# Last feed-forward of a graph network as one stage: scores as a row on TensorE, ranks between the chunks, weights last, stores by chunk

## The reference

```python
xn = _layernorm(x)                      # no gain, no bias
weights = (xn @ wr + br)[..., 0]        # one score per node
k = max(1, int(0.5 * s)); kk = k - 1    # 1561 nodes chosen
_, idx = jax.lax.top_k(weights, k)
sel_idx = idx[:, :kk]
h = jax.nn.gelu(sel @ w1 + b1)          # sel: the chosen rows of xn
y = (h @ w2 + b2) * weights[sel_idx]
x = x + (zeros.at[sel_idx].set(y) + xn)
```

## Time and profile before

| what | value |
|---|---|
| time, median of 3 executions | 7272.29 us (7267.86 to 7276.22) |
| the profiled execution: its own time, and its span | 7262.79 us, 7261.1 us |
| first instruction of the last feed-forward | 6856.65 us |
| part of the span from there | 404.5 us |
| TensorE busy over the span, mean granted clock | 4243.7 us, 0.806 |
| VectorE busy over the span | 3507.8 us |

### The profile page before, as it was taken

One profiled execution on the slowest core, in us unless ns is written; L12 is line 12 of the kernel. 1 busy time (PEld: TensorE's weight loads), 2 busy tenths in 40 slices (PEclk: granted clock), 3 DMA queues, 4 the chain that ended last, 5 costly groups with the idle time before them and its releaser, 6 DMA issues. The chain is left out here.

```text
span 7261.1 us, 68529 instructions
## 1 busy us (share of the span) xinstructions
PE 4243.7 (58%) x17811; PEld 2977.3 (41%) x17811; DVE 3507.8 (48%) x8561; ACT 1885.5 (26%) x4934; POOL 2998.9 (41%) x3029
## 2 busy tenths in 40 slices
PE   0022567777775693766664843554439964676428
PEld 0000334444443572334443642343228852454315
DVE  6800578888887313436453034632361115554461
ACT  0000056666664120023342110000012211443201
POOL 0677033333331364046662734666104433665200
PEclk9985678888887796878876976776759986988759
DMA  1001033333332373233334322334315642332200
GB/s 38 3 17 27 9 90 100 96 100 97 98 99 55 118 212 103 102 122 89 91 91 61 100 58 89 92 92 92 39 38 174 189 134 75 90 88 79 33 21 18
DMA packets 361250, 602.13 MB, mean 83 GB/s; under 512 B 119031, under 2 KB 245096, under 8 KB 357376
## 3 DMA queue, kind: packets, MB, share of 16 engines
q0 software_dynamic: 162496, 359.47, 20.5%
q1 hardware_dynamic: 198386, 238.43, 10.1%
HBM read 518.82 MB, written 78.64 MB: 82 GB/s over the span
## 5 line engine op out<-in xcount | busy, mean ns | idle before, releaser
L1665 POOL DMA_INDIRECT g0e_got<-g_table,g0e_rc x496 | 474.2, 956 | 1071.0 <-DVEq L1825 730.2
L1418 POOL DMA_INDIRECT g1e_got<-g_table,g1e_rc x496 | 491.0, 990 | 525.0 <-DMA g1e_rc<-rec_dst 294.1
L1418 POOL DMA_INDIRECT g2e_got<-g_table,g2e_rc x496 | 478.5, 965 | 338.8 <-issue 140.7
L1418 POOL DMA_INDIRECT g3e_got<-g_table,g3e_rc x440 | 430.9, 979 | 357.7 <-issue 117.4
L1474 PE MATMUL g2e_pa<-g2e_got,g2e_placew 128*125 128x256 f32 x992 | 341.8, 507 | 376.1 <-DVEq L1576 186.5
L250 POOL DMA_INDIRECT rec_dst<-bydst_rc,bydst_sloti x391 | 402.8, 1030 | 296.0 <-DVEq L442 175.4
L2628 PE MATMUL f_p<-f_w2s,f_hid 128*128 128x256 f32 (+1 forms) x2176 | 498.8, 386 | 43.4 <-ACT f_hid L2648 35.0
L1753 PE MATMUL g0e_spread<-g0e_expanded,g0e_by_tile 128*125 128x512 bf16 x992 | 417.1, 510 | 177.3 <-ACT g0e_spaced L1702 141.6
L2617 PE MATMUL f_p<-f_xt,f_w1s 128*128 128x256 f32 (+1 forms) x2176 | 493.7, 384 | 20.0 <-DMA f_b2s<-in_L_ffn_b 8.0
L1702 ACT ACTIVATE g0e_spaced<-g0e_spread 125x512 bf16<-125x512 f32 x992 | 499.4, 627 | 20.6 <-remote 7.4
L2648 ACT ACTIVATE f_hid<-f_p,f_b1s 128x256 f32<-128x256 f32 (+1 forms) x544 | 251.7, 471 | 861.0 <-PE f_p L2617 493.6
(11 more groups left out here) (656 smaller groups left out, 8265.3 us busy)
## 6 DMA issues: line engine op xcount, KB each, us to landing
f_w1s<-in_L_ffn_W SPq DMA_DIRECT2D x32, 1024.0 KB
f_w2s<-in_L_ffn_W SPq DMA_DIRECT2D x32, 1024.0 KB
g_table<-g1t_out SPq DMA_DIRECT2D x25, 1000.0 KB
f_w1s<-in_L_ffn_w SPq DMA_DIRECT2D x40, 512.0 KB
f_w2s<-in_L_ffn_w SPq DMA_DIRECT2D x40, 512.0 KB
f_results<-f_y SPq DMA_DIRECT2D x72, 256.0 KB
f_b2s<-in_L_ffn_b SPq DMA_DIRECT2D x80, 128.0 KB
f_rows<-XN SPq DMA_DIRECT2D x3, 3125.0 KB
```

Of the source, the lines that this page charges most:

```text
L1418: pool.indirect_dma_start(got[:, g % GOTS, j, :], None, table, bass.IndirectOffsetOnAxis(rc[:, g * GT + j, idx:idx + 1], 0))\
L1665: pool.indirect_dma_start(got[:, s, j, :], None, table, bass.IndirectOffsetOnAxis(rc[:, sl, j, R_IDX:R_IDX + 1], 0)).then_inc(got_in[s], 16)
```

## The change

The stages after the normalization become one block, `scored_experts_stage`, which also stores the result.

- All six loads are issued by SyncE in a small block ahead of `normalize_stage`.
- `wr` is spread over 125 identical columns (`wide`), so that a matmul with `wide` stationary and 500 columns of `XNT` moving leaves the row of 500 scores in each of 125 partitions: 14 matmuls in 7 chunks. VectorE adds the bias and writes `row`. The transpose and the way over DRAM are gone.
- `G` is taken out of `row` by a product with the identity, repeated 25 times, and a sum over each tile.
- TensorE starts the expert once all of `row` is out of PSUM. Between its chunks 0 to 4 VectorE places five tiles each (`place`: the rank instructions of before, and the `X += XN` of that tile), and then takes the chunk's four results with b2 into `XN` (`take`).
- After chunk 4 is taken the ranks are closed and `G` is masked; `settle` does `X += G * XN` for each tile. Chunks 5 and 6 are taken and settled tile by tile.
- SyncE stores each chunk of X when it is settled: six DMAs of 500 KB and one of 125 KB.
- The chunks are written out; there is no loop.

The removed lines of the rank computation, which stand in the function printed above, are cut here.

```diff
--- before.py
+++ after.py
@@ -3270,88 +3270,187 @@
                 pairs(dve, NT, add)
 
 
-def fourth_feed_forward(nc, R, a):
-    CAP = max(1, int(0.5 * N))
-    CHOSEN = CAP - 1 if CAP > 1 else 1
+def scored_experts_stage(nc, R, a, out, CHOSEN):
     F3 = a["L3_ffn_w1"].shape[1]
+    NF = F3 // 128
+    NQ = NCH + 1
+    RANKS = -(-NT // (NQ - 2))
     with ExitStack() as ctx:
         def sb(n, shape, dt=F32):
             return ctx.enter_context(nc.sbuf_tensor(f"f3_{n}", shape, dt))
 
...
+        w1s = sb("w1s", [128, KC, F3])
+        w2s = sb("w2s", [128, NF, D])
+        b1s = sb("b1s", [128, NF])
+        b2s = sb("b2s", [P, D])
+        wide = sb("wide", [128, KC, P])
+        G = sb("G", [P, NT])
+        row = sb("row", [P, N])
...
+        hid = sb("hid", [128, NF, CHUNK])
+        router_in, experts_in = sem("router_in"), sem("experts_in")
+        with nc.Block() as block:
+            @block.sync
+            def _(sp):
+                sp.dma_start(wr[:, :], a["L3_ffn_wr"]).then_inc(router_in, 16)
+                sp.dma_start(br[:, :], row_of(a["L3_ffn_br"], P)).then_inc(router_in, 16)
+                sp.dma_start(w1s[:, :, :], a["L3_ffn_w1"].rearrange("(c k) f -> k c f", k=128)).then_inc(experts_in, 16)
+                sp.dma_start(w2s[:, :, :], a["L3_ffn_w2"].rearrange("(c k) d -> k c d", k=128)).then_inc(experts_in, 16)
+                sp.dma_start(b1s[:, :], a["L3_ffn_b1"].rearrange("a k c -> (a k) c")).then_inc(experts_in, 16)
+                sp.dma_start(b2s[:, :], row_of(a["L3_ffn_b2"], P)).then_inc(experts_in, 16)
         normalize_stage(nc, R, "f3ln", R.X, R.XN)
-        add_stage(nc, [(R.X, R.XN)])
...
+        p1 = [ctx.enter_context(nc.psum_tensor(f"f3_p1{k}", [128, 512], F32)) for k in range(4)]
+        p2 = [ctx.enter_context(nc.psum_tensor(f"f3_p2{k}", [P, 512], F32)) for k in range(4)]
+        widened, scored, rowed, first, acted, second, taken, summed, stored = (sem(n) for n in (
+            "widened", "scored", "rowed", "first", "acted", "second", "taken", "summed", "stored"))
+        chunk = [(q * CHUNK, min(4, NT - 4 * q)) for q in range(NQ)]
+        with nc.Block() as block:
+            @block.tensor
+            def _(pe):
+                pe.wait_ge(widened, 1)
+                for q, (at, tiles) in enumerate(chunk):
+                    n = tiles * P
+                    if q >= 4:
+                        pe.wait_ge(rowed, q - 3)
+                    for c in range(KC):
+                        last = pe.matmul(p1[q % 4][0:P, 0:n], wide[:, c, :], R.XNT[:, c, at:at + n], start=(c == 0),
+                                         stop=(c == KC - 1))
+                    last.then_inc(scored, 1)
+                pe.wait_ge(experts_in, 64)
+                pe.wait_ge(rowed, NQ)
+                for q, (at, tiles) in enumerate(chunk):
+                    n = tiles * P
+                    for f in range(NF):
+                        m = q * NF + f
+                        if m >= 4:
+                            pe.wait_ge(acted, m - 3)
+                        for c in range(KC):
+                            last = pe.matmul(p1[f % 4][:, 0:n], w1s[:, c, f * 128:(f + 1) * 128], R.XNT[:, c, at:at + n],
+                                             start=(c == 0), stop=(c == KC - 1))
+                        last.then_inc(first, 1)
+                    pe.wait_ge(acted, (q + 1) * NF)
+                    for j in range(tiles):
+                        t = 4 * q + j
+                        if t >= 4:
+                            pe.wait_ge(taken, t - 3)
+                        for f in range(NF):
+                            last = pe.matmul(p2[j][:, 0:D], hid[:, f, j * P:(j + 1) * P], w2s[:, f, :], start=(f == 0),
+                                             stop=(f == NF - 1))
+                        last.then_inc(second, 1)
+            @block.scalar
+            def _(act):
+                act.wait_ge(experts_in, 64)
+                for q, (at, tiles) in enumerate(chunk):
+                    n = tiles * P
+                    if q > 0:
+                        act.wait_ge(second, 4 * q)
+                    for f in range(NF):
+                        act.wait_ge(first, q * NF + f + 1)
+                        act.activation(hid[:, f, 0:n], p1[f % 4][:, 0:n], ACT.Gelu_apprx_tanh, bias=b1s[:, f:f + 1])\
+                            .then_inc(acted, 1)
+            @block.vector
+            def _(dve):
+                dve.wait_ge(router_in, 32)
+                for c in range(KC):
+                    dve.tensor_scalar(wide[:, c, :], R.onesf[:, 0:P], wr[:, c:c + 1], None, ALU.mult)
+                dve.memset(rank[:, 1, 0:1], 0.0)
+                dve.drain().then_inc(widened, 1)
+                for q, (at, tiles) in enumerate(chunk):
+                    dve.wait_ge(scored, q + 1)
+                    dve.tensor_scalar(row[:, at:at + tiles * P], p1[q % 4][0:P, 0:tiles * P], br[:, 0:1], None, ALU.add)\
+                        .then_inc(rowed, 1)
+                dve.drain()
+                eye = R.identf[0:P, 0:P].rearrange("p (a n) -> p a n", a=1).broadcast_to([P, NT, P])
+                diagonal = ge[:, 0, :].rearrange("p (t n) -> p t n", n=P)
+                dve.tensor_tensor(diagonal, row[:, :].rearrange("p (t n) -> p t n", n=P), eye, ALU.mult)
+                dve.drain()
+                dve.tensor_reduce(G[:, :], diagonal, AX.X, ALU.add)
+                dve.drain()
+                def place(t):
+                    k = t % 2
+                    mine = G[:, t:t + 1]
+                    at = t * P
+                    if t > 0:
+                        dve.tensor_scalar(ge[:, k, 0:at], row[:, 0:at], mine, 0.0, ALU.is_ge, ALU.add,
+                                          accum_out=rank[:, 1, t:t + 1])
+                    dve.tensor_scalar(ge[:, k, at:N], row[:, at:N], mine, 0.0, ALU.is_gt, ALU.add,
+                                      accum_out=rank[:, 0, t:t + 1])
+                    dve.tensor_scalar(own[:, k, :], row[:, at:at + P], mine, None, ALU.is_equal)
+                    x = node_tile(R.X, t)
+                    dve.tensor_tensor(x, x, node_tile(R.XN, t), ALU.add)
                     dve.drain()
-                    for part in range(2):
-                        dve.tensor_tensor(rank[:, 2, :], rank[:, 2, :], rank[:, part, :], ALU.add)
-                        dve.drain()
-                    dve.tensor_scalar(rank[:, 2, :], rank[:, 2, :], float(CHOSEN), None, ALU.is_lt)
+                    dve.scalar_tensor_tensor(out=own[:, k, :], in0=R.upto[0:P, 0:P], scalar=0.0, in1=own[:, k, :],
+                                             op0=ALU.is_equal, op1=ALU.mult)
                     dve.drain()
-                    dve.tensor_tensor(G[:, :], G[:, :], rank[:, 2, :], ALU.mult)
-        experts_stage(nc, R, "f3", 1, F3, a["L3_ffn_w1"].rearrange("(a d) f -> a d f", a=1), a["L3_ffn_b1"],
-                      a["L3_ffn_w2"].rearrange("(a f) d -> a f d", a=1), a["L3_ffn_b2"].rearrange("(a d) -> a d", a=1), G,
-                      R.X[:, :], ACT.Gelu_apprx_tanh)
+                    dve.tensor_reduce(rank[:, 2, t:t + 1], own[:, k, :], AX.X, ALU.add)
+                def take(t):
+                    dve.wait_ge(second, t + 1)
+                    dve.tensor_tensor(node_tile(R.XN, t), p2[t % 4][:, 0:D], b2s[:, :], ALU.add).then_inc(taken, 1)
+                def settle(t):
+                    x = node_tile(R.X, t)
+                    return dve.scalar_tensor_tensor(out=x, in0=node_tile(R.XN, t), scalar=G[:, t:t + 1], in1=x,
+                                                    op0=ALU.mult, op1=ALU.add)
+                dve.wait_ge(experts_in, 64)
+                for q in range(NQ - 2):
+                    for t in range(q * RANKS, min((q + 1) * RANKS, NT)):
+                        place(t)
+                    for j in range(4):
+                        take(4 * q + j)
+                dve.drain()
+                for part in range(2):
+                    dve.tensor_tensor(rank[:, 2, :], rank[:, 2, :], rank[:, part, :], ALU.add)
+                    dve.drain()
+                dve.tensor_scalar(rank[:, 2, :], rank[:, 2, :], float(CHOSEN), None, ALU.is_lt)
+                dve.drain()
+                dve.tensor_tensor(G[:, :], G[:, :], rank[:, 2, :], ALU.mult)
+                dve.drain()
+                for q in range(NQ):
+                    for t in range(4 * q, 4 * q + chunk[q][1]):
+                        if q >= NQ - 2:
+                            take(t)
+                            dve.drain()
+                        settle(t)
+                    dve.drain().then_inc(summed, 1)
+            @block.sync
+            def _(sp):
+                rows = out.rearrange("(t p) d -> p t d", p=P)
+                for q, (at, tiles) in enumerate(chunk):
+                    sp.wait_ge(summed, q + 1)
+                    sp.dma_start(rows[:, 4 * q:4 * q + tiles, :],
```

(28 more changed lines are left out.)

## The result

The changed kernel takes 7076.36 us (7069.44 to 7078.77, 4 executions) against 7274.26 for the kernel before (4 executions): ratio 0.9728, 95% interval 0.9712 to 0.9743. The profiled execution took 7078.77 us with a span of 7077.1; the prediction had 7077.8 and, for the span, about 7076.

A forecast was written before the change was run, and what follows sets the result against it. One engine at a time bounds the last stages. Terms -159.6 + 3.4 - 3.2 - 25.6 = -185.0 us gave 7077.8 us for the profiled execution and 7087 for the median, 8 in 10 within 7080 to 7101.

The forecast's parts named there:

- carry the gain over to the median: Whole kernel: the 185.0 us gain, summed against the profiled 7262.79 us, was applied to the median of 7272.29.
- Loads in front: Block of six SyncE loads ahead of normalization: 3.4 us exposed cost, bounds 2.9 and 10.4.
- Stretch taken out: From normalization to the expert's first matmul: 12.0 us instead of 171.6, gain 159.6.
- Cover: Ranks, adds, closing and settles on VectorE under the expert's TensorE chunks of 28.33 us: nothing shows, priced at 0.
- The limit of 5.3: Placing on VectorE: up to 5.3 us per tile stays hidden; above that, each 0.1 us costs 2.5 us.
- Clock: TensorE at the expert's start: full clock expected, gaining the 3.2 us lost before.
- the rival: Low clock through the scores: they take 10.5 us more, the expert loses 3.2 again; 7101 us, chance 0.07.
- Store: Storing X by chunks at the end: 3.8 us after the last sum instead of 29.4, gain 25.6.
- the waiting block: Block of loads ahead of normalization waits for its data: 7 us more, 7094 us, chance 0.07.
- VectorE as the bound: In the expert's chunks, ranks lengthen beside TensorE to 6 or 8 us per tile: 7105 to 7155 us, chance 0.04.
- TensorE at 1.2 GHz throughout: No-gain rival: scores and expert last twice as long, 189 us more, 7276 us, chance 0.01.
- a slower kernel: TensorE waits for `taken` in each chunk: from 12.7 us per tile; about 7305 us at 14; chance 0.01.

The follow-up runs named there:

- before_b: The kernel before, run again unchanged in a later set on one chip: median 7310.15 us.
- heavy1000: Changed kernel with one more count over 1000 columns in the placing of each tile: last feed-forward's stage 236.60 us, 15.6 more.
- after_b: The changed kernel, run again unchanged on the chip of before_b: median 7119.66 us, ratio 0.9739 to the kernel before.
- after_dram: Changed kernel with the row buffer in DRAM back, kept by one small store ahead of the loads: 7116.60 us, ratio 0.9735 to the kernel before.

## Why the prediction was wrong, point by point

- **The step that failed** is the one from the profiled execution to the median: "carry the gain over to the median", with a range made from "the 4 us by which executions differ". The 4 us came from three executions. Eleven on one chip (before_b) spread over 17 us, and the trace I started from was of the kernel before at 7262.79, below all four executions of its first median. How far the untouched part moves between executions was left out. The sum itself hit the stage within 0.5 us: 185.0 against 184.5. That it also hit the whole profiled execution within 1 us, 7077.8 against 7078.77, is partly luck: in this pair the untouched parts ended within 0.5 us of each other, in the three later pairs 6.8 to 9.0 apart. With five executions of after against fifteen of before, medians are 7083.62, 7119.66 and 7116.49 on their chips, 187.7, 190.5 and 185.8 under before; any of these, taken off 7272.29, lies inside the range. In the first set it was 197.9, and the range had 7 us below the forecast where 10.6 were needed. Whether a part of the excess is real stays open.
- Terms of the sum: the misses are 0.7 us at most and partly cancel. Two stand outside it: the normalization took 0.2 us more, and the rest of the expert 0.5 less, mostly by chunks of 28.26 instead of 28.33.
- Loads in front: forecast 3.4, measured 4.1, mostly since the sixth issue took 1.29 us.
- Stretch taken out: forecast 12.0 for what replaces it. Measured from 6882.90 to 6894.98: 12.1 (0.57 to the first score, 10.76, 0.75).
- Cover: forecast that nothing of ranks, add, closing and settles shows. Right; no wait for `taken`, and chunks of 28.26. `place` was 4.77 against 4.78. The limit of 5.3 was right in size by luck: the late stores and not a late take make it.
- Clock: full, as forecast. The expert's first group took 13.66 us instead of 16.64, 3.0 gained where 3.2 was forecast. The price put on the rival was five times too high: I had the 500-column matmuls raise the clock in chunk 0 of the earlier trace rows and then did not let them do it in the scores. By that row it was 3.2; 2.7 was measured. The Trainium skill, in TensorE: Matmul & The Clock Gate, A second HAM failure mode, warns of swings where TensorE goes round PSUM banks with brief idle times. This trace shows none: going round four banks with idle times of up to 0.8 us, TensorE had a granted clock of 1.00 in every window from 6883.00 to 7072.50.
- Store: forecast 3.8 after the last sum, measured 3.55, so 25.8 gained where 25.6 was forecast. With the fixed 2.0 us that the Trainium skill (DMA: Bandwidth & Descriptors, Anatomy of one DMA) gives for DMAs issued by GpSimd, the estimate would have been 3.2; the measured value lies between the two.
- Rivals: the waiting block did not occur and was priced rightly (7.1 measured). VectorE as the bound, TensorE at 1.2 GHz throughout and a slower kernel did not occur.

## What to carry to other kernels

When a stage is one engine after another, first ask which single engine has to do the most, and put the rest between its pieces in the order in which results are asked for: here the same ranks, all placed ahead of the takes, cost 85 us more. When work moves under a cover, look for the next thing that starts when it ends: the stores could start only when the ranks were closed, and in heavy1000 they, not TensorE, set most of the delay. And compare a change of a few microseconds by the length of its own stage in the traces; the whole time of such a program is a wide ruler.

## What the runs showed of the hardware that I had not expected

The same program takes very different times on different chips: the kernel before 6801.21 and 6804.51 us on two of them (one execution each), and 7271.33, 7302.24 and 7310.15 on three others. The difference lies ahead of the last feed-forward, for the most part in stretches that hold the graph layers with their gathers; whether the gathers or the chips are its cause was not tried. heavy1000, on one of the faster chips, has the same two rows as above:

```profile
L476 DVE BATCH_NORM_STATS2 f2ln_stats<-XN x25: 407/409/427, 5001.1 to 5009.0; 125x6 f32<-125x256 f32 x25
L476 DVE BATCH_NORM_STATS2 f3ln_stats<-X x25: 407/409/427, 6388.5 to 6396.3; 125x6 f32<-125x256 f32 x25
```

1387.4 us instead of 1489.8, both with the block of loads (the second is after_b). Between the two normalizations of the third feed-forward, a stretch without gathers, pass 61.9 us in after_b and in heavy1000. The last feed-forward, which has no gathers either, shows none of it: on those two chips the stages came out at 246.5 and 228.1, within 0.2 us of the changed kernel's 221.0 plus the later end of the store (29.0 - 3.55) and the longer idle time (12.49 - 5.22). A DMA issue by SyncE, 0.3 to 0.6 us in the earlier trace rows, took 1.20 to 1.38 us as the sixth in a row in all the runs that have that row, and 1.46 as the seventh in after_dram. It was the load of b2, whose issue took 0.60 as the fourth in a row before; why it grows was not tried.
